# Four shared PSUM banks, VectorE masks and a new order in a four-layer attention kernel

## The chip, the core and the metric

The kernel runs on one core of one Trainium2 chip. The metric is the device time of one execution in microseconds. The core's engines are TensorE (PE in the rows, with its weight loads as PEld), VectorE (DVE), ScalarE (ACT), GpSimd (POOL) and SyncE (SP), which issues most of the DMAs. Matmul results go to PSUM, which has eight banks of 128 partitions by 512 f32; everything else is in SBUF.

## What is computed

Four layers work on x of 8 batches x 256 tokens x 256 features, with a context tensor of the same shape. Each layer adds cross attention (16 heads of 16) and then a feed-forward part to x:

```
x = x + L0_xattn(layernorm(x), ctx)          # causal, strict
x = x + layernorm(x) @ sign(W)
x = x + L1_xattn(layernorm(x), ctx)          # causal
x = x + L1_moe(layernorm(x))                 # 16 experts, top 2, 2 shared
x = x + L2_xattn(ctx, layernorm(x), mask)    # mask of keys, q/k/v normed
x = x + L2_bitlinear_ffn(layernorm(x))       # gate, up, down, quantised
x = x + L3_xattn(layernorm(x), ctx, ctx)     # no weights, no mask
x = x + L3_qlora_ffn(layernorm(x))           # 3 blocks: linear, layernorm, gelu, linear, add
```

An attention is softmax(q k^T / 4 + mask) v for each head. In layer 2 a masked score is replaced by -1e9 in the reference; the kernel adds -1e30 instead.

## The kernel before

**Attention.** A pair of layer and batch, (L, b), is one slot of 16 heads. `ORDER` lists the 32 slots: 16 of layers 0 and 1 mixed, then (2,0) to (2,3), then layer 3 and layer 2 in turn, then the last of layer 3. For each head, TensorE makes the scores twice. The first time (`maxima`, `score_for_max`, L1545) they lie with queries on partitions, and VectorE takes each row's negated maximum from them (`reduce`). These maxima are split into two bf16 parts (L2207, L2209), turned on TensorE (`turn_max`, L1630) and copied by ScalarE as extra rows under the stacked queries (`rows`, L1976). The second time (`score`, `score_for_exp`, L1563) the scores lie with keys on partitions and have the maximum already subtracted; ScalarE takes the exponential (`exp`, L1959), and TensorE multiplies by the values (L1649). Queries and keys are split into three bf16 parts, whose six combinations are stacked on 96 rows by six DMAs each (`q_stack`, `k_stack`, L2789): the high part needs ScalarE alone (`q_hi`), the middle one VectorE as well, the low one GpSimd last. Eight further rows of `k_st` hold ones that pick a head's maximum (`own_rows`, L1983).

**Masks.** In the causal layers VectorE adds a triangle while it takes the maximum: a custom instruction for each half of the keys (L2192), each followed by a read of its accumulator. In layer 2 TensorE adds the mask to the first scores, as one more matmul of an identity by `mask_s`, 512 columns (L1548), and again to the second ones (L1569); VectorE then takes both maxima of a head with one plain reduction (L2196).

**PSUM.** `claim` gives a tile one of the banks of its use: scores ("s") have banks 0 and 1, maxima ("m") banks 2 and 3, all else ("c") banks 4 to 7, with a loan from "m" when 4 to 7 are planned to be full. It takes the bank whose holder is planned to be drained first, and TensorE waits for that drain, in order.

**Norms.** VectorE makes mean and variance (L2090, L2093), GpSimd var+eps, -mean, its power -1/2 and the shift (L2503, L2504, L2506, L2509), ScalarE applies scale and shift (L1910; for the last batch's halves `half_apply`, L2051), TensorE turns the tile. The last batch's three blocks of layer 3 run as two halves of 128 tokens (`last_half`).

**Order.** All engines run through one list of steps: the table `AT` gives each step of each lane a planned time, and `program` visits the steps in the order of those times. Each engine issues its own part of every step in that order. At the start SyncE loads context and x of batch 0, weights for keys and queries, `col`, the value weights and so on; GpSimd makes the constants (`constants`: fills, triangles, numbers) before its first norm; SyncE's zero fills of a scratch table in DRAM (L2839) stand between the first stacks.

## Time and profile before

| | us |
|---|---|
| median of 3 runs (lowest to highest) | 1173.37 (1168.38 to 1174.31) |
| profiled execution, own time | 1173.09 |
| its span, first to last instruction | 1171.4 |
| PE busy in the span | 1061.8 (91%) |
| VectorE busy | 886.7 (76%) |
| ScalarE busy | 810.9 (69%) |
| GpSimd busy | 554.4 (47%) |

A group's busy time is the union of its instructions from start to end. Instructions of TensorE, and of VectorE and ScalarE, overlap: the next one may start before the one ahead has ended, so a row's mean duration is more than it takes of the engine when work is queued. The distance from one start to the next, read from a timeline, is called the pitch below.

### The profile page before, as it was taken

What the parts mean: (1) busy time and instruction counts of PE and PEld (TensorE: products, weight loads), DVE (VectorE), ACT (ScalarE), POOL (GpSimd) and SP (SyncE); (2) the same over time, 40 slices, a digit from 0 to 9 for tenths busy, and PEclk for the clock granted to TensorE, in tenths of its full rate; (3) what the DMA queues carried; (4) which work ended last, traced back from release to release, by engine and by line L of the source; (5) the groups of instructions that cost most, each with busy time, mean ns of one, the idle gap of its engine ahead of it and who ended that gap; (6) DMA issues with size and microseconds to landing.
All of it is one profiled execution on the core that took longest, in us unless ns stands there. A gap on an engine that the chain in (4) does not pass through costs nothing.

```text
span 1171.4 us, 25960 instructions
## 1 busy us (share of the span) xinstructions
PE 1061.8 (91%) x8406; PEld 787.6 (67%) x8406; DVE 886.7 (76%) x2995; ACT 810.9 (69%) x1492; POOL 554.4 (47%) x1111
## 2 busy tenths in 40 slices
PE   5899999999999989888999997899998999889986
PEld 4577777787787867766767664566575765656664
DVE  2898887788465669987847588998888969898643
ACT  5676666666665557566566666567988897899963
POOL 7132364655212456687812126746455445344244
PEclk9899999999999999999999999999999999999898
DMA  8884332225677552522368853322123111322000
GB/s 279 243 287 146 91 92 65 80 74 155 189 217 215 162 151 64 145 73 89 119 194 256 252 186 101 93 62 84 45 75 108 38 55 47 90 64 55 1 19 18
DMA packets 102324, 140.01 MB, mean 120 GB/s; under 512 B 12336, under 2 KB 79792, under 8 KB 102192
## 3 DMA queue, kind: packets, MB, share of 16 engines
q1 hardware_dynamic: 99120, 129.97, 37.8%
q0 software_dynamic: 3072, 8.39, 2.3%
q8 instruction: 70, 1.15, 0.4%
q14 instruction: 62, 0.51, 0.2%
HBM read 65.43 MB, written 22.54 MB: 75 GB/s over the span
## 4 chain that ended last, share of the span: by engine, by line
PE 41%; DVE 22%; ACT 14%; DMA 7%; issue 7%; SPq 5%; POOL 4%; another core or an unknown queue 1%; DVEq 0%; ACTq 0%; POOLq 0%
PE ps L1525 9%; PE ps L1563 4%; PE ps L1649 4%; DVE neg_max L2196 4%; PE ps L1545 4%; DMA w<-in_expert 3%; ACT probs L1959 3%; PE ps L1742 3%; PE ps L1518 3%; DVE ps L2192 2%; PE ps L1532 2%; SPq L2789 2%; DVE bn L2090 2%; ACT q_st L1976 2%; PE ps L1709 2%
## 5 line engine op out<-in xcount | busy, mean ns | idle before, releaser
L1959 ACT ACTIVATE probs<-ps 128x384 f32<-128x384 f32 (+1 forms) x512 | 260.3, 544 | 90.2 <-PE ps L1566 43.5
L1545 PE MATMUL ps<-k_st,q_st 96*128 96x256 bf16 (+1 forms) x1024 | 170.6, 262 | 23.4 <-DVE neg_max L2196 11.8
L1563 PE MATMUL ps<-q_st,k_st 104*128 104x256 bf16 (+1 forms) x1024 | 177.1, 261 | 12.9 <-ACT probs L1959 8.4
L2196 DVE TENSOR_REDUCE neg_max<-ps 128x2 f32<-128x512 f32 x256 | 167.7, 679 | 15.7 <-PE ps L1548 8.9
L1976 ACT ACTIVATE q_st<-ps 8x1024 bf16<-8x1024 f32 x128 | 129.7, 1016 | 42.2 <-PE ps L1630 38.9
L2192 DVE CUSTOM_DVE_ANT_0 ps<-ps,diag_s 128x128 f32<-128x128 f32 (+1 forms) x384 | 123.0, 357 | 29.6 <-PE ps L1545 26.4
L1545 PEld LDWEIGHTS ps<-k_st,q_st 96*128 96x128 bf16 x1024 | 85.4, 98 | 76.4 <-DVE neg_max L2196 23.8
L2503 POOL TENSOR_SCALAR var_eps<-mv 128x2 f32<-128x2 f32 (+1 forms) x115 | 30.7, 267 | 210.1 <-DVE mv L2093 203.2
L1563 PEld LDWEIGHTS ps<-q_st,k_st 104*128 104x128 bf16 x1024 | 90.6, 99 | 58.5 <-ACT probs L1959 20.8
L1649 PE MATMUL ps<-probs,v 128*32 128x256 f32 (+1 forms) x2048 | 122.6, 358 | 2.9 <-ACT probs L1959 1.8
L2569 POOL CAST parts<-qf 128x512 bf16<-128x512 f32 x64 | 39.5, 618 | 115.9 <-DVE qf L2115 57.6
L1649 PEld LDWEIGHTS ps<-probs,v 128*32 128x32 f32 x2048 | 54.4, 109 | 48.3 <-issue 22.6
L2506 POOL TENSOR_TENSOR rstd<-var_eps,neg_half 128x2 f32<-128x2 f32 (+1 forms) x115 | 84.1, 731 | 0.0
L2571 POOL TENSOR_TENSOR parts<-qf,parts 128x512 bf16<-128x512 f32 x64 | 74.5, 1165 | 5.2
L1525 PE MATMUL ps<-w,xn_t 128*128 128x256 f32 x296 | 72.5, 388 | 2.6 <-ACT xn_t L1867 2.4
L1910 ACT ACTIVATE xn<-x,shift,rstd 128x256 f32<-128x256 f32 x112 | 64.1, 633 | 13.8 <-POOL shift L2509 8.0
L1742 PE MATMUL ps<-ring,w 128*128 128x128 f32 x496 | 65.7, 278 | 8.2 <-DMA w<-in_expert 8.1
L2192 DVE DVE_READ_ACCUMULATOR2_ANT neg_max<- 128x1 f32 x512 | 71.8, 140 | 0.0
L1742 PEld LDWEIGHTS ps<-ring,w 128*128 128x128 f32 x496 | 60.9, 191 | 15.2 <-issue 13.8
L1566 PE MATMUL ps<-diag_t,ident_b 128*128 128x256 bf16 x256 | 70.3, 275 | 0.0
L1525 PEld LDWEIGHTS ps<-w,xn_t 128*128 128x128 f32 x296 | 54.4, 193 | 13.0 <-issue 5.5
L1525 PE MATMUL ps<-w,ctx_t 128*128 128x256 f32 x256 | 61.4, 384 | 0.0
(270 smaller groups left out, 2516.3 us busy)
## 6 DMA issues: line engine op xcount, KB each, us to landing
k_st<-parts SPq DMA_DIRECT2D x192, 128.0 KB, 2.4
q_st<-parts SPq DMA_DIRECT2D x192, 128.0 KB
w<-in_expert SPq DMA_DIRECT2D x62, 384.0 KB, 3.9
x_rows<-wo SPq DMA_DIRECT2D x10, 768.0 KB, 7.6
ctx_t<-in_ctx_t SPq DMA_DIRECT2D x16, 256.0 KB, 3.6
ring<-x_rows SPq DMA_DIRECT2D x31, 128.0 KB, 3.4
y_rows<-ring SPq DMA_DIRECT2D x31, 128.0 KB, 3.5
xn_t<-x_rows SPq DMA_DIRECT2D x31, 128.0 KB, 4.0
```

Source lines behind the costliest of these rows:

```text
L1525: last = mm(t[:, a * D:(a + 1) * D], act_t[:, kt, a * P:(a + 1) * P], weight[:, kt, :], start=kt == 0, stop=kt == KT - 1)
L1545: last = mm(t[:, c0:c0 + n], head(q_st, r, h, KROWS, j * P, P), head(k_st, r, h, KROWS, 0, n), start=j == 0 or L != 2, stop=L != 2, skip_g ...
L1563: last = mm(t[:, j * S:j * S + n], head(k_st, r, h, KALL, j * P, P), head(q_st, r, h, KALL, skip, n), start=j == 0 or L == 3, stop=L == 3, ...
L1566: last = mm(t.rearrange("p (j t) -> p j t", j=SJ)[:, :, 0:P], ident_b[:, :], diag_t[:, L, :, :], start=False, stop=True, skip_group_check= ...
L1649: last = mm(t[h4 * DPAD:(h4 + 1) * DPAD, skip:S], v[:, r, j, hg * HPG + h4, :], probs[:, (hg % 2) * HPG + h4, j * S:(j + 1) * S - skip], s ...
L1742: last = mm(t[:, n * P:(n + 1) * P], expert[:, i % RING, c0:c0 + INNER_E], x_tile_t[:, i % 2, kt * P:(kt + 1) * P], start=kt == 0, stop=kt ...
L1959: nc.scalar.activation(probs[:, (hg % 2) * HPG + h4, 0:width], tile_of(key)[:, 0:width], ACT.Exp, scale=SCALE).then_inc(*tile_drained(key))
L1976: nc.scalar.activation(out, tile_of(key)[KROWS:KALL, 0:S].unsqueeze(1).to_broadcast([2 * HPG, HPG, S]), ACT.Copy).then_inc(*tile_drained(key))
L2192: last = V.tensor_tensor_reduce(some, some, diag_s[:, n0:n0 + j * step + 1:step, :], -1.0, -NEG, ALU.add, ALU.min, neg_max[:, hg, h4, j:j ...
L2196: V.tensor_reduce(neg_max[:, hg, h4, :], tile_of(key).rearrange("p (j t) -> p j t", j=SJ), AX.X, ALU.max, negate=True).then_inc(*tile_drai ...
L2506: G.tensor_tensor(rstd[:, kind, tiles], var_eps[:, kind, tiles], neg_half[:, 0:SJ if a is None else 1], ALU.pow).then_inc(*ln_rstd.step((p ...
L2571: G.tensor_tensor(parts[:, 2, n, :, :], rest, parts[:, 1, n, :, :], ALU.subtract).then_inc(*part_lo.step((what, L, b)))
```

## The change

1. `banks`: "s" and "m" both have banks 0 to 3; a loan for "c" may be any of the four.
2. `MASKED_BY_V = range(8)`: in every batch of layer 2 the mask matmul of the first scores is gone, and VectorE adds `mask_s` with the custom instruction, two for each head.
3. At the start: `col` is loaded ahead of the query weights; ten matmuls on the identity (`EARLY`) run before the first product; the three high parts of the first query stack are issued from ScalarE's DMA queue (`stack_hi`); `own_rows` wait for the first query's high part; GpSimd makes the first norm's factors before the triangles, and the numbers after the first query split; context and x of batch 2 are loaded after that split.
4. `apply_by_v` and `half_apply_by_v`: the norm ahead of the last batch's blocks and the norms in its six half blocks are applied by VectorE from mean and power; GpSimd's -mean and shift are gone there.
5. A new table `AT` with other times for all steps.

```diff
+MASKED_BY_V = range(8)
+EARLY = 10
+NORMED_BY_V = {("l3f", LAST)}
...
 def constants(part):
     yield
     part.constants()
+    yield
+    part.masks_causal()
+    yield
+    part.numbers()
...
-        banks = {"s": (0, 1), "m": (2, 3), "c": (4, 5, 6, 7)}
+        banks = {"s": (0, 1, 2, 3), "m": (0, 1, 2, 3), "c": (4, 5, 6, 7)}
...
             pe.wait_ge(*const_ready.at("half"))
+            for _ in range(EARLY):
+                mm(ps[:, 7, 0:P], ident[:, :], ident[:, :], start=True, stop=True)
...
+                    by_pe = L == 2 and b not in MASKED_BY_V
                     last = mm(t[:, c0:c0 + n], head(q_st, r, h, KROWS, j * P, P), head(k_st, r, h, KROWS, 0, n),
-                              start=j == 0 or L != 2, stop=L != 2, skip_group_check=L == 2)
-                if L == 2:
+                              start=j == 0 or not by_pe, stop=not by_pe, skip_group_check=by_pe)
+                if by_pe:
                     last = mm(t, ident_b[:, :], mask_s[:, b % 2, :, :].rearrange("p j t -> p (j t)"),
                               start=False, stop=True, skip_group_check=True)
...
+            def stack_hi():
+                act.wait_ge(*part_hi.at(("q", *ORDER[0])))
+                for at in range(NSPLIT):
+                    if SPLIT_Q[at] == 0:
+                        nc.scalar.dma_start(q_st[at:KROWS:NSPLIT, side(*ORDER[0]), :, :, :].rearrange("d h m t -> d (h m t)"),
+                                            parts[:, 0, PART["q"], :, :].rearrange("p m t -> p (m t)")).then_inc(
+                            *hi_stacked.step(at))
...
                 def own_rows(r):
+                    act.wait_ge(*part_hi.at(("q", 0, 0)))
...
+            def norm_tile(p, b, a, out, src):
+                T = b * SJ + a
+                V.tensor_scalar(out, src, mv[:, 0, T, 0:1], rstd[:, 0, T:T + 1], ALU.subtract, ALU.mult).then_inc(
+                    *norm_by_v.step((p, b, a)))
...
+                    elif L == 2 and b in MASKED_BY_V:
+                        if h == 0:
+                            dve.wait_ge(*mask_ready.at((b, 0)))
+                        for j in range(SJ):
+                            some = tile_of(key)[:, j * S:(j + 1) * S]
+                            last = V.tensor_tensor_reduce(some, some, mask_s[:, b % 2, j, :], -1.0, -NEG,
                                                           ALU.add, ALU.min, neg_max[:, hg, h4, j:j + 1])
                         last.then_inc(*tile_drained(key))
...
+                by_v = a is not None or (p, b) in NORMED_BY_V
+                if not by_v:
+                    G.tensor_scalar(neg_mean[:, kind, tiles], mv[:, kind, tiles, 0], -1.0, None, ALU.mult).then_inc(*ln_mean.step((p, b)))
...
             load_batch(0, 0)
+            load_x(0)
             load_weight(W_L0K)
+            sp.dma_start(col[:, :, :].rearrange("p n k -> p (n k)"), col_d).then_inc(*load["col"].step(0))
             load_weight(W_L0Q)
-            sp.dma_start(col[:, :, :].rearrange("p n k -> p (n k)"), col_d).then_inc(*load["col"].step(0))
```

TensorE at the start, before. `ctx_t` is the context turned, `xn` the normed x, `xn_t` the same turned; the product of `xn_t` and w is the query.

```order
L1518 MATMUL ps<-ctx_t,w 128x256 x4
L1525 MATMUL ps<-w,ctx_t 128x256 x8
L1532 MATMUL ps<-ident,xn 128x128 x4
L1518 MATMUL ps<-ctx_t,w 128x256 x4
L1518 MATMUL ps<-xn_t,w 128x256 x4
L1518 MATMUL ps<-ctx_t,w 128x256 x4
```

TensorE at the start, after:

```order
L1534 MATMUL ps<-ident 128x128 x10
L1539 MATMUL ps<-ctx_t,w 128x256 x4
L1553 MATMUL ps<-ident,xn 128x128 x4
L1539 MATMUL ps<-ctx_t,w 128x256 x4
L1539 MATMUL ps<-xn_t,w 128x256 x4
L1546 MATMUL ps<-w,ctx_t 128x256 x8
L1553 MATMUL ps<-ident,xn 128x128 x4
```

The eight value products (w, ctx_t) stood ahead of the first query product and now stand behind it.

VectorE where layer 2 begins, before. The ISA rows are the custom instruction and the read of its accumulator; `w` holds a token tile here.

```order
L2209 TENSOR_TENSOR max_parts<-neg_max,max_parts 128x2x4
L2196 TENSOR_REDUCE neg_max<-ps 128x2 x2
L2219 RECIPROCAL sum_inv<-ps 128x16
L2222 TENSOR_TENSOR o_tok<-ps,sum_inv 128x2x128
L2196 TENSOR_REDUCE neg_max<-ps 128x2
L2097 TENSOR_TENSOR w<-ps,vec 128x512
```

The same place, after:

```order
L2257 TENSOR_TENSOR max_parts<-neg_max,max_parts 128x2x4
L2240 ISA ps,neg_max<-ps,mask_s 128x256
L2240 ISA neg_max 128x1
L2240 ISA ps,neg_max<-ps,mask_s 128x256
L2240 ISA neg_max 128x1
L2135 TENSOR_TENSOR w<-ps,vec 128x512
```

One reduction of a head has become two custom instructions with two reads, and the token tile's bias comes after the first head and not the third.

TensorE near the end, in layer 3's last slots, before (L1545 is a product for maxima, L1563 one for scores; two of them are one head):

```order
L1545 MATMUL ps<-k_st,q_st 128x256 x4
L1525 MATMUL ps<-w 128x256 x4
L1563 MATMUL ps<-q_st,k_st 128x256 x2
L1660 MATMUL ps<-ident,o_raw 128x128 x4
L1545 MATMUL ps<-k_st,q_st 128x256 x4
```

The same stretch, after (L1567 for maxima, L1585 for scores):

```order
L1585 MATMUL ps<-q_st,k_st 128x256 x2
L1675 MATMUL ps<-probs,v 32x256 x8
L1567 MATMUL ps<-k_st,q_st 128x256 x10
L1553 MATMUL ps<-ident,ring 128x128 x4
L1686 MATMUL ps<-ident,o_raw 128x128 x4
```

No run of one kind was longer than two heads before; now there are runs of three to five heads.

## Rows read from the trace of the kernel before

**Rows 1.** Windows: us; busy and count by engine; granted clock; DMA share; GB/s

```profile
0.00:50.00 50.00, 33.47 (x200) 25.43 (x201) 23.09 (x111) 27.07 (x42) 26.03 (x66) 0.90 0.95 292
50.00:500.00 450.00, 424.75 (x3702) 341.70 (x3702) 345.75 (x1605) 287.94 (x590) 202.10 (x430) 1.00 0.48 140
500.00:700.00 200.00, 185.98 (x1418) 138.00 (x1417) 142.63 (x411) 127.11 (x262) 91.11 (x203) 1.00 0.56 168
700.00:1000.00 300.00, 271.01 (x2028) 179.31 (x2028) 261.71 (x597) 238.74 (x385) 162.92 (x273) 0.98 0.26 74
1000.00:1100.00 100.00, 92.48 (x764) 63.88 (x764) 87.35 (x205) 91.33 (x144) 38.21 (x70) 0.98 0.19 53
1100.00:1171.40 71.40, 54.09 (x299) 39.30 (x297) 26.20 (x72) 38.72 (x73) 34.00 (x71) 0.90 0.04 16
```

**Rows 2.** Windows of L1548 (mask matmuls) alone: us; PE and PEld busy

```profile
500.00:700.00 200.00, 24.30 (x64) 6.14 (x64) 1.00 0.56 168
700.00:1000.00 300.00, 24.82 (x64) 6.27 (x64) 0.98 0.26 74
```

**Rows 3.** Groups by form: count, then busy us, mean ns, idle before

```profile
L2192 DVE DVE_READ_ACCUMULATOR2_ANT neg_max<- 128x1 f32 x512 | 71.8, 140 | 0.0
```

**Rows 4.** Timeline of PE: start, us, what, count

```profile
905.28 0.38 PE L1548 MATMUL ps<-mask_s,ident_b 128*128 128x512 bf16 x1
905.50 2.21 PE L1781 MATMUL ps<-w,xn_t 128*128 128x512 bf16 x8
```

**Rows 5.** Timeline of VectorE, a causal head and a plain reduction

```profile
94.93 0.47 DVE L2192 CUSTOM_DVE_ANT_1 ps<-ps,diag_s 128x256 f32<-128x256 f32 x1
95.31 0.14 DVE L2192 DVE_READ_ACCUMULATOR2_ANT neg_max<- 128x1 f32 x1
95.31 0.33 DVE L2192 CUSTOM_DVE_ANT_0 ps<-ps,diag_s 128x128 f32<-128x128 f32 x1
...
946.52 0.68 DVE L2196 TENSOR_REDUCE neg_max<-ps 128x2 f32<-128x512 f32 x1
947.11 0.68 DVE L2107 TENSOR_TENSOR qf<-qf,parts 128x512 f32<-128x512 f32 x1
```

**Rows 6.** Waits, whole span: total us, times, longest

```profile
PE ps L1545 <- DVE neg_max L2196: 11.8, 19, 1.5
...
PE ps L1742 <- DMA w<-in_expert: 8.1, 11, 1.4
...
PE ps L1563 <- ACT probs L1959: 8.4, 11, 2.2
```

**Rows 7.** Timeline of the first 29 us

```profile
5.43 0.12 POOL L2482 MEMSET score<- 128x32 f32 x1
...
6.64 3.51 PE L1518 MATMUL ps<-ctx_t,w 128*128 128x256 f32 x8 [6.64 <-DMA w<-in_w]
...
10.81 0.19 POOL L2509 TENSOR_TENSOR shift<-neg_mean,rstd 128x2 f32<-128x2 f32 x1
...
15.61 1.89 PE L1518 MATMUL ps<-xn_t,w 128*128 128x256 f32 x8
...
19.30 3.88 ACT L1983 ACTIVATE k_st<-own 8x1024 bf16<-8x1024 bf16 x4
19.30 6.04 SPq L2789 DMA_DIRECT2D q_st<-parts  x6
...
28.01 0.49 PE L1545 MATMUL ps<-k_st,q_st 96*128 96x128 bf16 x4 [0.26 <-DMA q_st<-parts]
```

**Rows 8.** Timeline of one half block's norm near the end

```profile
1160.28 0.57 POOL L2506 TENSOR_TENSOR rstd<-var_eps,neg_half 128x1 f32<-128x1 f32 x1
...
1160.92 0.19 POOL L2509 TENSOR_TENSOR shift<-neg_mean,rstd 128x1 f32<-128x1 f32 x1
1161.15 0.60 ACT L2051 ACTIVATE w<-w,shift,rstd 128x256 f32<-128x256 f32 x1 [3.04 <-POOL shift L2509]
```

**Rows 9.** Groups by form: the nearest forms of a VectorE norm

```profile
L2394 DVE TENSOR_SCALAR xn_t<-xn 128x256 bf16<-128x256 f32 x16 | 4.9, 351 | 0.0
```

More of the change, by code:

```diff
@@ L760, in norm @@
     yield
-    part.apply(p, b)
+    if (p, b) in NORMED_BY_V:
+        part.apply_by_v(p, b)
+    else:
+        part.apply(p, b)
     yield
@@ L1131, in last_half @@
         yield
-        part.half_apply(n, a)
+        part.half_apply_by_v(n, a)
         yield
@@ L1357, in normed_of, with wait_hi_stacked @@
             return h_of(b) if p == "l3f" else xn[:, NORMED[p], :, :]
+        def wait_hi_stacked(eng):
+            eng.wait_ge(*hi_stacked.at(max(at for at, part in enumerate(SPLIT_Q) if part == 0)))
         def half(a):
@@ L1876, in split_hi @@
                     act.wait_ge(*stacked[what][side(*order[-1])].at((*order[-1], NSPLIT - 1)))
+                    if what == "q" and order[-1] == ORDER[0]:
+                        wait_hi_stacked(act)
                 order.append((L, b))
@@ L1923, in q_hi @@
                     split_hi("q", L, b)
+                    if (L, b) == ORDER[0]:
+                        stack_hi()
                 def token_hi(what, b):
@@ L2155, in v_take @@
                 def v_take(L, b):
+                    if L == 0 and b < 2:
+                        dve.wait_ge(*const_ready.at("v"))
                     before = same_side_before(L, b)
@@ L2456, in half_bias, with half_apply_by_v, apply_by_v @@
                     V.bn_aggr(mv[:, 0, T, :], bn[:, 0, T, :]).then_inc(*ln_moments.step((("y", n), LAST, a)))
+                def half_apply_by_v(n, a):
+                    dve.wait_ge(*ln_rstd.at((("y", n, a), LAST)))
+                    y = y_set(LAST)[0][:, a, :]
+                    norm_tile(("y", n), LAST, a, y, y)
+                def apply_by_v(p, b):
+                    dve.wait_ge(*ln_rstd.at((p, b)))
+                    for a in range(SJ):
+                        norm_tile(p, b, a, normed_of(p, b)[:, a, :], x[:, b * SJ + a, :])
                 def half_add(n, a):
@@ L2783, in stack @@
                     wait_filled(sp, ("s", *before, HG - 1, HPG - 1))
-                n = 0
+                n = split.count(0) if (what, L, b) == ("q", *ORDER[0]) else 0
                 for part, ready in enumerate((part_hi, part_mid, part_lo)):
+                    if part == 0 and n:
+                        continue
                     sp.wait_ge(*ready.at((what, L, b)))
```

36 lines of the change are left out of this document (24 added, 12 removed), and 1054 rows, old and new, of the table AT.

## The prediction

> **What bounds the kernel now.** I read the windows first, since the shares of the whole span hide that the stretches differ [rows 1]. From 50 to 500 us TensorE is busy 94% of the time and VectorE 77%. From 500 to 700, where layer 2's first four batches lie beside the experts, TensorE is busy 93%, VectorE 71% and ScalarE 64%: TensorE alone is full. From 700 to 1000, with the other four batches of layer 2, TensorE has 90%, VectorE 87% and ScalarE 80%; from 1000 to 1100 the three have 92%, 87% and 91%. There no engine is far ahead, and a lighter TensorE soon meets the two others. The first 50 us keep TensorE busy for 33.5 only, with the DMA engines at 0.95, and the last 71.4 for 54.1: these two ends are chains of dependent steps. Then I read the timelines, because a busy TensorE is not a TensorE at its peak. A mask matmul starts at 905.28 and lasts 0.38 us, yet the next matmul starts at 905.50 [rows 4]: in a queue it takes 0.22 us. VectorE overlaps in the same way: a custom instruction over 256 columns starts at 94.93, the next one at 95.31, and the accumulator's read lies beside that next one; a plain reduction over 512 columns starts at 946.52 and what follows it at 947.11 [rows 5]. So the pitches are 0.38 and 0.59 us.
>
> **Masks on VectorE.** TensorE loses 64 matmuls in each of the two stretches [rows 2], at 0.22 us each 14.1 us, 28.2 in all. The recorded durations would make it 49.1, the sum of the two busy times, which is an upper bound that the pitch speaks against. VectorE's price is read from the causal head, since the trace has no such instruction in layer 2: the form is the same, PSUM in and out with a bf16 operand beside it. A head goes from 0.59 to 2 x 0.38 = 0.76 us, 0.17 more, and for 128 heads 21.8 us, 10.9 in each stretch. The upper end takes all durations in a row: 2 x (0.47 + 0.14) - 0.68 = 0.54 a head, 69 us in all [rows 3, 5]. The lower end is zero, since the custom form touches every score that the reduction touches. I take the pitch, the nearest row.
>
> What of this is on the path depends on the stretch. From 500 to 700 VectorE's 142.6 us become 153.5 and stay well under TensorE, whose 186.0 fall to 171.9. I let three quarters of the 14.1 shorten the stretch, -10.5; the rest goes to waits for expert weights, of which TensorE has 8.1 us in all already [rows 6]. From 700 to 1000 VectorE would have 261.7 + 10.9 = 272.6 of 300 and TensorE 256.9, so VectorE becomes the fullest engine. Here I count a quarter of TensorE's gain and a quarter of VectorE's load: -3.5 + 2.7 = -0.8. The sum is -11.3, with ends of -28 (all of TensorE's time comes off, VectorE costs nothing) and +11 (nothing comes off, VectorE's second half counts in full).
>
> Here two pages of the Trainium skill give other prices. The page "TensorE: Matmul & The Clock Gate", section "Back-to-back issue gap", gives about 131 ns as the sustained spacing of matmuls with 512 columns; by that the 128 masks would be worth 16.8 us and the whole forecast would come out some 5 us later. The trace does not agree: it shows 0.22 us, in a stream of eight further matmuls of 512 columns too, 2.21 us for eight. The other page's rule stands with the first rival.
>
> **Shared banks.** TensorE's own waits that this can touch are those for VectorE's maxima, 11.8 us, and for ScalarE's exponentials, 8.4 us [rows 6]. With four banks a run of three to five heads of one kind can be in flight where two could be. But a wait ends when the reader is done, and more banks don't make the reader faster; what they remove is the part due to uneven runs. I take a fifth, -4. The ends are -20 (both waits gone) and +8: TensorE claims in order, by planned drain times, and a bank held by a late exponential can now stop a product for maxima, which at worst doubles the shorter of the two waits. Nothing is added behind such a wait but TensorE's own queue.
>
> **The start.** The chain to the first maxima now: the first product begins at 6.64 with the key weights' landing; the first norm's factors are ready at 11.0, although GpSimd ends its fills at 5.55 and needs some 1.5 us for them; the query product runs from 15.61 to 17.5, behind the eight value products; SyncE issues the six query stacks from 19.30 to 25.34; the first maxima start at 28.01, when the last stack has landed [rows 7]. After: the factors are ready near 7.2; ScalarE applies them while the first product runs, TensorE turns x at about 10.3, makes the second key product, and the query product ends near 14. That is 3.4 us earlier. Three of six stacks leave from ScalarE, so SyncE issues three, some 3 us instead of 6. The first maxima could start at 21 to 22, 6 to 7 us earlier. The zero fills that filled the DMA engines during the second stack come later. What it costs: ScalarE makes its eight `own_rows` in one piece, twice the 3.88 us of the row, and the norm of batch 1 and the exponentials queue behind its three DMA issues and these rows; the fills and weights still have to move, with the DMA engines at 0.95 now. I take -5 of the 7; the ends are -8 and 0. The ten early matmuls lie in time in which TensorE waits for weights. Eight products took 3.51 us at 6.64 and 1.89 at 15.61, near the ratio of the clock's two levels (2.4 and 1.2 GHz), so if the early ones raise the clock the first product ends up to 1.6 us sooner; that is inside the ends. The triangles are due only at the first maxima, and about 2.5 us of GpSimd's work hides beside the first products.
>
> **The end.** In a half block GpSimd's power ends at 1160.85, the shift at 1161.11 and ScalarE's norm at 1161.75, 0.90 us after the power [rows 8]. VectorE's norm has no row; the nearest is a tensor_scalar of the same 128x256 from f32 at 351 ns [rows 9], with bounds of 0.3 (its pitch) and 0.6 (as slow as ScalarE). With 0.1 for the hand-over it ends 0.45 after the power, and the power starts 0.18 earlier without -mean: 0.63 saved. Four such norms stand one after another (the one ahead of the blocks, three blocks), -2.6, with ends -4 and 0. VectorE is busy 26 of 71 us there, so it has the room; its adds for the other half queue behind the wait for the power, which they need anyway.
>
> **Sum.** -11.3 - 4 - 5 - 2.6 = -22.9 against the profiled execution's own 1173.09, which lies 0.3 from the median: 1150.2 us.
>
> **Rival 1, VectorE becomes the bound (slower).** If a masked head costs the durations and not the pitch, 0.54 us more, then VectorE has 261.7 + 34.6 = 296 us to do from 700 to 1000. It is at 87% there now; at 90% that takes 329 us, +29. With -5 from 500 to 700, -5 at the start and -2.6 at the end it is +16: 1189. It decides from about 0.35 us more a head. For it: a new read of the accumulator sits ahead of every split of the maxima. Against it: the overlap in [rows 5]. The page "VectorE: DVE Perf Modes", section "The DRAIN you can't avoid", says that the next VectorE instruction does not start until the pipe is empty; by that rule this rival would hold, but the trace shows the next one 0.09 us ahead of the recorded end. I give it 0.12.
>
> **Rival 2, the middle is bound by more than TensorE.** The mask matmuls go, and ScalarE, VectorE and the expert weights keep their pace, so that only the ends move: -5 - 2.6 = -7.6, 1165.5. For it: ScalarE at 80 to 91% after 700 and VectorE at 87%. Against it: 500 to 700, where TensorE alone is full. 0.19.
>
> **Rival 3, the change does not do what it says.** The earlier start is lost by 50 us because the same loads and fills are only moved, and longer runs of one kind make the banks a wait in turn, +8 against the masks' -11: the sum is about -3, 1170. For it: the DMA share at the start. 0.07.
>
> **How the numbers follow.** The forecast, 1150.2, has a chance of 0.62, and its own range from the terms' ends is 1132 to 1163. Rival 2 spreads over 1161 to 1171. The range 1132 to 1176 takes in the forecast, rivals 2 and 3 and leaves out rival 1 and a little on both sides. A measurement of this kernel tells about 0.5%, 5.9 us, from no change. Faster by more: 0.62 of the forecast and 0.11 of rival 2, 0.73. Within: 0.08 of rival 2 and 0.07 of rival 3, 0.15. Slower: 0.12.
>
> **What would show it.** In the new profile the first maxima start near 21.5 us; a masked head on VectorE has custom starts 0.38 apart; the matmul count is 128 lower but for ten; the stretch that held 500 to 700 is some 10 us shorter and that of 700 to 1000 hardly; VectorE is over 90% there; from the last exponential to the end 2 to 4 us are gone. A start of the maxima after 26, a head at 1.2 us, or a TensorE wait for maxima above 20 us would each break one step. What would make it wrong as a whole is the new table: it moves every step, and a place where an engine's order no longer fits what is ready costs several us at once and shows in no single row of before.

## The result and the profile after

The changed kernel takes **1195.19 us** (median of 4 runs, 1192.96 to 1199.67) against 1173.84 of before: a ratio of 1.0173, 95% interval 1.0134 to 1.0212. It is 21 us slower where the forecast said 23 faster and put its top end at 1176. The profiled execution has its own time of 1192.96 us and a span of 1191.2.

Time is compared here at equal work. Each head has one exponential, 512 in all, 16 to a slot; their numbers from 0 mark how far a kernel has come. Windows of before and then of after, each from exponential 0 to 256 (layers 0 and 1), from 256 to the last (layers 2 and 3, the experts), and from the last to the end; columns as in [rows 1]:

```profile
35.80:518.40 482.60, 451.14 (x3948) 359.60 (x3946) 373.16 (x1724) 309.45 (x629) 219.39 (x472) 0.99 0.49 145
518.40:1116.90 598.50, 549.01 (x4173) 380.92 (x4171) 481.00 (x1165) 460.33 (x793) 286.64 (x521) 0.98 0.34 100
1116.90:1171.40 54.50, 38.90 (x193) 28.90 (x191) 20.89 (x56) 24.07 (x50) 25.64 (x57) 0.93 0.04 15
```

```profile
30.60:538.80 508.20, 462.45 (x3949) 365.58 (x3949) 372.50 (x1745) 307.59 (x632) 221.92 (x477) 0.98 0.48 143
538.80:1139.90 601.10, 521.00 (x4008) 363.37 (x4047) 499.24 (x1520) 459.12 (x790) 286.28 (x522) 0.99 0.35 100
1139.90:1191.20 51.30, 36.84 (x184) 27.95 (x184) 23.07 (x59) 19.90 (x42) 21.90 (x40) 0.97 0.04 16
```

The first exponential comes 5.2 us earlier and the last stretch is 3.2 shorter, as forecast. But layers 0 and 1, where behind the start only the banks and the order differ, take 25.6 us more for the same matmuls (3948 and 3949): TensorE idles 45.8 of 508.2 us instead of 31.5 of 482.6, and its busy time grows by 11.3. In the second stretch TensorE is busy 28.0 us less, and the stretch is 2.6 us longer: all of it became idle time. That this is just the 28.2 that the masks were priced at is in part chance, since order and clock differ too. Where the masks are the only difference in the program, the same stretch has 542.44 us of TensorE in e2 and 521.00 in after, 21.4 less, and 549.01 in before and 534.29 in e9 (below), 14.7 less at a lower clock.

The waits of TensorE in after over the whole span (total us, times, longest), the rows that answer to [rows 6] and the largest others:

```profile
PE ps L1553 <- ACT xn L1946: 8.5, 9, 2.4
PE ps L1656 <- DVE max_parts L2257: 7.5, 14, 1.3
PE ps L1567 <- DMA q_st<-parts: 7.3, 4, 3.7
PE ps L1768 <- DMA w<-in_expert: 6.7, 10, 1.5
PE ps L1585 <- DVE neg_max L2240: 6.1, 8, 2.3
PE ps L1585 <- DVE neg_max L2232: 5.7, 11, 1.2
PE ps L1585 <- ACT probs L1997: 5.5, 11, 1.3
PE ps L1567 <- DVE neg_max L2240: 4.9, 11, 1.4
```

L1553 turns the normed x, L1656 the maxima's parts, L1768 is a product of the experts, L1567 the product for maxima, L1585 the scores' product, L2232 and L2240 VectorE's causal and masked maxima. That L1585 waits for VectorE's maxima is new, since the two kinds now share their banks: before has no such row, while e5, with the banks alone, has 1.4 us of them and after 14.0. All of TensorE's waits for VectorE's maxima together are 16.2 us in before and 23.1 in after; over 20 was the prediction's own sign that a step had broken. The longest wait of these rows is 3.7 us. Summed over all rows of this view by the engine waited for, TensorE waits in before for VectorE 30.8 us in 61 waits, for ScalarE 41.4 in 64 and for DMAs 20.5 in 19; in after for VectorE 61.5 us in 107 waits, for ScalarE 45.0 in 69 and for DMAs 15.7 in 16.

**The new table forecasts the direction itself.** Its times are tenths of a microsecond of the planner's own model. Exponential 256 is planned at 4969 in the old table and at 5065 in the new one, the last at 10715 and 10783: 9.6 us and 6.8 us later by the plan's own account, and its last step is 3.7 us later. Measured are 20.4, 23.0 and, at the end, 19.9.

### The profile page after: what moved, and what is told of

It is laid out like the page before. It is cut to its first block, busy times and chain, and to the rows that moved or that the text cites. A ratio compares the mean times of both kernels' runs of the same rounds, so it can differ in the third digit from the quotient of the medians.

```text
span 1191.2 us, 26150 instructions
## 1 busy us (share of the span) xinstructions
PE 1043.8 (88%) x8257; PEld 776.1 (65%) x8298; DVE 908.9 (76%) x3387; ACT 804.2 (68%) x1484; POOL 551.1 (46%) x1097
## 4 chain that ended last, share of the span: by engine, by line
PE 39%; DVE 26%; ACT 11%; issue 8%; DMA 6%; POOL 5%; SPq 4%; another core or an unknown queue 0%; DVEq 0%; POOLq 0%; ACTq 0%
PE ps L1546 9%; PE ps L1675 4%; DVE ps L2232 4%; PE ps L1585 4%; PE ps L1768 3%; PE ps L1567 3%; ACT probs L1997 3%; DVE ps L2240 3%; PE ps L1539 3%; DVE bn L2123 2%; DMA w<-in_expert 2%; PE ps L1553 2%; SPq L2863 2%; DVE neg_max L2244 2%; PE ps L1775 2%
## 5 line engine op out<-in xcount | busy, mean ns | idle before, releaser
L1997 ACT ACTIVATE probs<-ps 128x384 f32<-128x384 f32 (+1 forms) x512 | 256.4, 548 | 75.6 <-PE ps L1588 31.4
L1585 PE MATMUL ps<-q_st,k_st 104*128 104x256 bf16 (+1 forms) x1024 | 172.4, 262 | 26.6 <-DVE neg_max L2240 6.1
L1567 PE MATMUL ps<-k_st,q_st 96*128 96x256 bf16 (+1 forms) x1024 | 156.8, 264 | 24.2 <-DMA q_st<-parts 7.3
L2014 ACT ACTIVATE q_st<-ps 8x1024 bf16<-8x1024 f32 x128 | 129.6, 1016 | 54.5 <-PE ps L1656 48.9
L2232 DVE CUSTOM_DVE_ANT_0 ps<-ps,diag_s 128x128 f32<-128x128 f32 (+1 forms) x384 | 123.0, 360 | 25.8 <-PE ps L1567 21.2
L1585 PEld LDWEIGHTS ps<-q_st,k_st 104*128 104x128 bf16 x1024 | 89.2, 99 | 72.5 <-issue 20.3
L1567 PEld LDWEIGHTS ps<-k_st,q_st 96*128 96x128 bf16 x1024 | 84.9, 99 | 71.9 <-issue 21.4
L2240 DVE CUSTOM_DVE_ANT_0 ps<-ps,mask_s 128x256 f32<-128x256 f32 x256 | 101.1, 453 | 10.7 <-PE ps L1567 8.9
L2244 DVE TENSOR_REDUCE neg_max<-ps 128x2 f32<-128x512 f32 x128 | 82.7, 680 | 11.7 <-PE ps L1567 11.6
L1675 PEld LDWEIGHTS ps<-probs,v 128*32 128x32 f32 x2048 | 54.9, 109 | 52.2 <-issue 28.1
L1768 PE MATMUL ps<-ring,w 128*128 128x128 f32 x496 | 66.3, 279 | 8.7 <-DMA w<-in_expert 6.7
L2232 DVE DVE_READ_ACCUMULATOR2_ANT neg_max<- 128x1 f32 x512 | 72.5, 142 | 0.0
L1768 PEld LDWEIGHTS ps<-ring,w 128*128 128x128 f32 x496 | 61.0, 191 | 14.9 <-issue 11.6
```

Of the source, the lines that this page charges most:

```text
L1567: last = mm(t[:, c0:c0 + n], head(q_st, r, h, KROWS, j * P, P), head(k_st, r, h, KROWS, 0, n), start=j == 0 or not by_pe, stop=not by_pe, ...
L1585: last = mm(t[:, j * S:j * S + n], head(k_st, r, h, KALL, j * P, P), head(q_st, r, h, KALL, skip, n), start=j == 0 or L == 3, stop=L == 3, ...
L1675: last = mm(t[h4 * DPAD:(h4 + 1) * DPAD, skip:S], v[:, r, j, hg * HPG + h4, :], probs[:, (hg % 2) * HPG + h4, j * S:(j + 1) * S - skip], s ...
L1768: last = mm(t[:, n * P:(n + 1) * P], expert[:, i % RING, c0:c0 + INNER_E], x_tile_t[:, i % 2, kt * P:(kt + 1) * P], start=kt == 0, stop=kt ...
L1997: nc.scalar.activation(probs[:, (hg % 2) * HPG + h4, 0:width], tile_of(key)[:, 0:width], ACT.Exp, scale=SCALE).then_inc(*tile_drained(key))
L2014: nc.scalar.activation(out, tile_of(key)[KROWS:KALL, 0:S].unsqueeze(1).to_broadcast([2 * HPG, HPG, S]), ACT.Copy).then_inc(*tile_drained(key))
```

## The experiments

All are timed against runs of before on the same chip, four chips in all. The mean granted clock differs from run to run, and the time goes with it: 95 runs of before lie between 0.969 and 0.987, and their time falls by 8.0 us for each 0.01 (correlation -0.81). So the table has two columns of differences to before: of the medians, and from one straight-line fit over the runs of all kernels (8.1 us for each 0.01), with 95% bounds: the difference that is left when the clock is the same. Where a change itself lowers the clock, as is seen below, the last column leaves that part of its cost out, so both are needed.

| kernel | median us | ratio, 95% | difference | clock, median | at equal clock |
|---|---|---|---|---|---|
| after | 1195.19 | 1.0173, 1.0134 to 1.0212 | +21.4 | 0.974 | +17.9 ± 2.3 |
| e1 after, old order | 1184.58 | 1.0073, 1.0042 to 1.0104 | +9.1 | 0.970 | +4.1 ± 1.6 |
| e2 after, masks by TensorE | 1200.11 | 1.0192, 1.013 to 1.0254 | +24.6 | 0.978 | +24.5 ± 2.3 |
| e3 new order and banks | 1207.18 | 1.0255, 1.0188 to 1.0321 | +31.7 | 0.981 | +32.7 ± 2.3 |
| e4 masks alone | 1183.06 | 1.0055, 1.003 to 1.008 | +7.6 | 0.971 | +1.8 ± 1.6 |
| e5 banks alone | 1173.06 | 0.9982, 0.9953 to 1.001 | -1.8 | 0.981 | +0.3 ± 1.4 |
| e6 end alone | 1174.30 | 1.0005, 0.9969 to 1.0041 | -0.5 | 0.978 | -0.9 ± 1.4 |
| e7 new order only from 257 on | 1184.53 | 1.0071, 1.004 to 1.0102 | +9.7 | 0.978 | +7.9 ± 1.5 |
| e8 as e1, masks by TensorE | 1183.00 | 1.0042, 1.0008 to 1.0076 | +8.2 | 0.974 | +3.0 ± 1.5 |
| e9 no masks on either engine | 1176.13 | 1.0007, 0.9981 to 1.0034 | +0.3 | 0.972 | -3.6 ± 1.5 |
| e10 masks on both engines | 1183.69 | 1.0085, 1.0058 to 1.0113 | +7.8 | 0.976 | +7.5 ± 1.4 |
| e11 VectorE masks four batches | 1178.08 | 1.0035, 1.0006 to 1.0064 | +2.2 | 0.975 | +2.5 ± 1.4 |
| e12 new order up to 256 | 1198.33 | 1.023, 1.017 to 1.029 | +22.5 | 0.968 | +16.8 ± 2.2 |
| e13 new order up to 128 | 1188.50 | 1.0137, 1.0066 to 1.0208 | +12.0 | 0.972 | +9.9 ± 2.3 |
| e14 new order 128 to 256 | 1200.77 | 1.0219, 1.0148 to 1.029 | +24.2 | 0.966 | +16.2 ± 2.5 |
| e15 start and end | 1176.80 | 0.9998, 0.9968 to 1.0028 | +0.3 | 0.978 | +1.1 ± 1.5 |
| e16 banks and end | 1171.90 | 0.997, 0.993 to 1.0009 | -4.6 | 0.980 | -1.5 ± 1.5 |

And the start of some exponentials in the profiled executions, in us in before and as differences to it. Each row is one execution: that of e4 is 3.5 us slower than its median, that of e1 4.7 faster.

| kernel | 0 | 16 | 64 | 128 | 160 | 256 | 448 | last | end |
|---|---|---|---|---|---|---|---|---|---|
| before | 35.8 | 56.3 | 127.0 | 240.4 | 289.9 | 518.4 | 1008.9 | 1116.9 | 1171.4 |
| after | -5.3 | +0.4 | +9.6 | +4.8 | +13.7 | +20.4 | +21.9 | +23.0 | +19.9 |
| e1 | -5.2 | +0.4 | +0.5 | 0.0 | +0.5 | +1.4 | +9.5 | +7.1 | +6.8 |
| e3 | 0.0 | +6.4 | +16.0 | +12.2 | +19.1 | +24.7 | +32.3 | +33.0 | +33.8 |
| e4 | +0.2 | -2.6 | -2.5 | -3.2 | -4.0 | -3.0 | +14.9 | +13.2 | +13.5 |
| e12 | -5.1 | -3.8 | +5.9 | +5.2 | +12.7 | +17.6 | +24.2 | +21.9 | +21.6 |
| e14 | -5.3 | +1.1 | +1.2 | +2.9 | +13.8 | +18.8 | +28.5 | +26.1 | +25.8 |

**First four: which part costs.** T1 held that the masks and banks pay and the order takes it away; T2 that the masks cost as well.

e1: the changed kernel with the order of before from the 9th exponential on. The old times are shifted to join the new start, so that no step changes its place behind it.

```diff
-    (267, 278, 287, 291, 296, 300, 304, 328, 376, 379, 382, 385, 407, 410, 413, 416, 483, 489, 497, 502, 518, 521, 524, 527,
+    (267, 278, 287, 291, 296, 300, 304, 328, 376, 379, 379.004, 379.008, 379.019, 394, 397, 410, 431, 434, 444, 447, 480,
```

> The changed kernel whole (four shared banks, masks on VectorE, new start, VectorE's last norms), but the steps stand in the order of the table of before from the ninth exponential on; only what lies ahead of it keeps the new order. Theory 1, the new order is what costs: the time falls from 1195 to 1155 to 1170, and the first half (up to the 257th exponential, 538.8 us in the changed kernel, 518.4 before) ends before 522. Theory 2, the masks or the shared banks cost under any order: the time stays at 1185 to 1200.

e2:

```diff
-MASKED_BY_V = range(8)
+MASKED_BY_V = ()
```

> The changed kernel with layer 2's masks made by TensorE again for all eight batches, nothing else. Theory 1, the order costs and the masks are worth little either way: 1189 to 1201, and the first half is as in the changed kernel, 538 to 540 us. Theory 2, the masks on VectorE cost: 1180 or less. The prediction's own step (masks on VectorE save 11 us) expects 1206.

e3: the kernel before with the new table and the shared banks. In e5 the same line of banks is all that differs from before.

```diff
-        banks = {"s": (0, 1), "m": (2, 3), "c": (4, 5, 6, 7)}
+        banks = {"s": (0, 1, 2, 3), "m": (0, 1, 2, 3), "c": (4, 5, 6, 7)}
```

> The kernel before with two things alone: the new table and the four shared banks (the new table's runs of one kind don't fit two banks). The start, the masks and the last norms are as before. Theory 1, the order costs: 1190 to 1205, with the first half ending 18 us or more later than before's 518.4. Theory 2, other parts cost: within 8 us of before's 1173.

e4: the kernel before with VectorE's masks.

```diff
+                    by_pe = L == 2 and b not in MASKED_BY_V
...
-                if L == 2:
+                if by_pe:
```

> The kernel before with one thing alone: VectorE adds layer 2's masks. Theory 1 takes the masks for nearly free or a small gain: 1163 to 1176. Theory 2, they cost: 1180 or more. The prediction's step expects 1162.

The old order takes 11 us off the changed kernel (e1) and the new one adds over 30 to before (e3): the order is the largest cost. But e1 is still 9 us slower than before, and the masks alone make before 7.6 us slower (e4). Under the new order the same masks are worth -4.9 (e2 against after; with four runs of each this is clear of zero only at equal clock, -6.6 ± 3.2). So the parts don't simply add, and T1 is half right: it fails on the masks. At equal clock e4's loss is 1.8 ± 1.6: most of the 7.6 comes with a lower clock.

**Second four: banks, end, the second half of the order.**

> The kernel before with nothing changed but the banks: scores and maxima share four. Theory A (the new order is what costs in layers 0 and 1; shared banks cost nothing by themselves): with the old order the exponential number 256 starts within 2 us of before (518.4), the time is 1168 to 1176. Theory B (the shared banks are the loss in layers 0 and 1, since a bank held by a late exponential stops a product for maxima): number 256 starts 10 us or more later and the time is 1183 or more. The prediction's step said -4, with ends of -20 and +8.

e6, with the norm ahead of the blocks changed in the same way:

```diff
-        part.half_apply(n, a)
+        part.half_apply_by_v(n, a)
```

> The kernel before with the last norms on VectorE and nothing else changed. From the last exponential to the end before takes 54.5 us. Theory A (each of the four norms in the chain is shorter by about 0.6 us): 51 to 52.5, the time 1170 to 1172. Rival (the chain is bound by GpSimd's power and VectorE's statistics, so the norm's engine does not matter, and the 51.4 us of after come from elsewhere): 54 to 55 us, time as before within 1 us.

e7, from the second lane of the table (the exponentials) around number 256, against the new table:

```diff
-4985, 5004, 5018, 5065, 5097, 5102, 5107
+4843, 4856, 4860, 4910.012, 4910.023, 4910.028, 4910.03
```

> The changed kernel in full, but from the 9th to the 256th exponential with the order of before, and from the 257th on with the new order. Theory A (the new order costs about 24 us before exponential 256 and is better than the old one after it, where it is 598 to 601 us against 604 in e1): exponential 256 starts at 518 to 522 and the time is 1170 to 1178. Theory C (the cost of the new order is only put off, work left undone by then comes after it): 1185 or more.

e8: e1 with `MASKED_BY_V = ()`, as in e2.

> As e1_old_order (new start, shared banks, last norms on VectorE, order of before from the 9th exponential on), but TensorE adds layer 2's masks as before. Theory A (masks on VectorE cost here what they cost alone in e4 less what shared banks give back, 5 to 8 us, and the new start is worth nothing by 56 us): 1167 to 1174. Theory D (the masks are not the cost of e1; the new start or the banks are): 1180 or more.

Banks alone move exponential 256 by 0.9 us and the time by nothing that can be told: theory B falls. The end alone is worth 0.4 us from the last exponential to the end in the trace (54.1 us), not 2.6: that is e6's rival, and its theory A falls. e7 has exponential 256 at 519.2 as theory A said, but with 1184.5 it is above A's 1178 and just under C's 1185, and no better than e1 (3.8 ± 2.1 worse at equal clock): the new order behind exponential 256 brings nothing either. e8, 1183.0, is where theory D put it, 1180 or more: under the old order the masks are not the cost of e1, from which e8 differs by 1.6 us, 1.1 ± 2.0 at equal clock. Banks, start and end together cost 8.2 us, although banks alone (e5), end alone (e6) and start with end (e15, below) cost nothing that can be told. At equal clock 3.0 ± 1.5 are left of it; why they cost in company stays open.

**Third four: the masks taken apart, and the order.**

e9: VectorE's branch of e4 is never taken, and TensorE's matmuls stay away. e10: VectorE adds, and TensorE too. e11: half the batches.

```diff
-                    elif L == 2 and b in MASKED_BY_V:
+                    elif False:
```

```diff
-                    by_pe = L == 2 and b not in MASKED_BY_V
+                    by_pe = L == 2
```

```diff
-MASKED_BY_V = range(8)
+MASKED_BY_V = range(4)
```

> The kernel before, but layer 2's maxima are taken without the masks: neither TensorE's 128 mask matmuls nor VectorE's adds are done, VectorE keeps its plain reductions (what is left out: the mask's part of the maximum; the masks of the scores stay). The price of the matmuls by themselves. Theory E (after exponential 288 TensorE is not alone the limit: what it no longer does becomes waits for VectorE and ScalarE, and a lower clock): 1167 to 1176. Theory F (the prediction's: the pitch of 0.22 us comes off where TensorE is full): 1155 to 1163.

> The kernel before, TensorE adds layer 2's masks as before and VectorE adds them once more (a masked score is masked twice, the maximum is the same). VectorE's price with TensorE's load unchanged. Theory E (VectorE's queue is the limit after exponential 288, so TensorE's matmuls there are covered, and the clock stays as in before): as e4, 1178 to 1186, with a clock of 0.975 or more. Theory F (TensorE is the limit and VectorE's 0.17 us a head is mostly covered): 1175 to 1179 if e4's loss is not VectorE's; a time 8 us or more above e4 would say that the matmuls do sit on the path.

> The kernel before, with VectorE adding the masks of layer 2's first four batches only (64 heads, beside the experts, where VectorE is busy 71%). Theory E (the loss of e4 lies after exponential 384 or so, where VectorE is as full as TensorE; before it, VectorE has room): 1165 to 1174, clock 0.975 or more. Rival (any wait that TensorE gains lowers its clock, so this half costs as well): 1177 to 1181.

e12, the second lane around number 256, against the new table:

```diff
-4985, 5004, 5018, 5065, 5097, 5102, 5107
+4985, 5004, 5018, 5062.003, 5062.005, 5062.006, 5062.008
```

> The changed kernel in full, with the new order up to the 256th exponential and the order of before behind it: the counterpart of e7. Theory A (the new order's cost is made before exponential 256, about 20 us, and the old order behind it costs what it costs in e1, 604 us): exponential 256 at 538 to 541 and 1195 to 1202. Theory C (work is only shifted between the halves, so that halves from two orders cost at the seam as e7 may have): exponential 256 at 538 to 541, and 1185 to 1194.

This settles the masks. **In the old order, taking TensorE's 128 mask matmuls away brings nothing**: with them gone and nothing put in their place, the time is 1176.1 against 1175.9 (e9). VectorE's adds cost 7.8 us with TensorE's load unchanged (e10), and 7.3 with the matmuls gone (7.6 of e4 less 0.3 of e9). Windows from exponential 288 to 448, layer 2's masked heads beside experts and layer 3, of before, e9 and e4:

```profile
610.80:1008.90 398.10, 363.56 (x2759) 249.45 (x2760) 329.41 (x767) 304.47 (x521) 183.80 (x305) 0.99 0.37 108
```

```profile
613.40:1013.40 400.00, 352.21 (x2673) 240.20 (x2674) 332.01 (x767) 304.90 (x521) 184.09 (x305) 0.97 0.37 108
```

```profile
610.50:1023.90 413.40, 359.14 (x2641) 246.12 (x2674) 343.09 (x1025) 305.28 (x522) 184.28 (x305) 0.95 0.36 105
```

e9 has 86 matmuls fewer than before, TensorE's busy time falls by 11.4 us, its idle time grows by 13.3, and the clock goes from 0.99 to 0.97. In e4 the busy time hardly falls, although the matmuls are gone, since the others run at 0.95. Where that happens is seen in windows of 5 us at the same time, before and then e4; both start at exponential 320, and by 745 before has begun 332 and e4 328:

```profile
725.00:730.00 5.00, 2.94 (x29) 1.37 (x22) 4.83 (x11) 2.19 (x5) 3.56 (x5) 1.00 0.65 170
730.00:735.00 5.00, 2.98 (x21) 1.36 (x19) 4.76 (x12) 4.46 (x9) 4.63 (x8) 1.00 0.13 42
735.00:740.00 5.00, 4.63 (x45) 3.22 (x46) 4.72 (x10) 3.62 (x7) 4.01 (x5) 1.00 0.05 11
740.00:745.00 5.00, 5.00 (x52) 3.60 (x53) 4.90 (x11) 3.69 (x7) 3.28 (x4) 1.00 0.66 181
```

```profile
725.00:730.00 5.00, 2.73 (x27) 1.40 (x16) 4.83 (x11) 1.72 (x4) 4.01 (x5) 1.00 0.66 184
730.00:735.00 5.00, 2.54 (x15) 1.15 (x14) 4.79 (x10) 3.73 (x8) 4.70 (x8) 0.66 0.09 26
735.00:740.00 5.00, 4.60 (x33) 2.74 (x32) 4.79 (x9) 1.93 (x4) 2.17 (x3) 0.50 0.00 0
740.00:745.00 5.00, 5.00 (x20) 3.31 (x19) 3.61 (x6) 3.70 (x7) 2.01 (x2) 0.50 0.38 102
```

In both VectorE is busy 4.8 of 5 us for 10 us and TensorE only a little over half. In before TensorE's waits there are for VectorE, the two longest being these:

```profile
729.69 0.39 PE L1545 MATMUL ps<-k_st,q_st 96*128 96x256 bf16 x2 [1.48 <-DVE neg_max L2196]
731.92 0.39 PE L1545 MATMUL ps<-k_st,q_st 96*128 96x256 bf16 x2 [0.82 <-DVE neg_max L2196]
```

So VectorE is the bound there. In e4 TensorE is busy a little less still, and then its clock is granted at 0.50, 1.2 GHz, while its work comes back: 20 matmuls in 5 us instead of 52. The clock's part is carried by the timed runs too: with the matmuls kept it is 0.977 (before, same chip) and 0.976 (e10) in the median, with them gone 0.972 (e9) and 0.971 (e4). At equal clock the matmuls would be worth 3.6 us (e9 against before) to 5.7 (e4 against e10); the lower clock takes 0.005 x 8.1 us per 0.01, some 4, back. That fewer matmuls cause the lower clock rests on these pairs; e1 against e8 and after against e2 point the same way (0.971 and 0.974, 0.974 and 0.978), but not beyond their spread.

e11 shows that the first four batches cost too (+2.2), though VectorE has room there by the windows [rows 1]: the rival with its 1177 to 1181 is right, theory E's 1165 to 1174 wrong. e12 loses most of what after loses up to exponential 256 (+17.6 of +20.4), and then 4.0 more; its 1198.3 is theory A's.

**Last four: where the order costs.**

e13 and e14, the second lane around numbers 128 and 256, against the new table; e14 has the old order up to 128 as e1:

```diff
-2247, 2260, 2349, 2357, 2360, 2377, 2380
+2247.001, 2260, 2349, 2353.006, 2356, 2372, 2383
```

```diff
-4985, 5004, 5018, 5065, 5097, 5102, 5107
+4835, 4854, 4868, 4912.003, 4912.005, 4912.006, 4912.008
```

> The changed kernel in full, with the new order up to the 128th exponential only and the order of before behind it. The traces of after and e12 have gone 8 us back between exponentials 48 and 64 and then gained 2 to 5 again by 128. Theory G (the cost is spread, each part of the order carries its own, and what is behind by 128 stays behind): exponential 256 starts 3 to 8 us later than in e1 (519.8), time 1186 to 1192. Theory H (the loss by 128 is work drawn forward, which the old order behind it gets back): as e1, 1182 to 1186. Theory I (one late step early on makes all of the loss): 1195 or more.

> The changed kernel in full, with the new order from the 128th to the 256th exponential only. In after this stretch, from 240.4 + 4.8 to 518.4 + 20.4, is 15.6 us longer than in before, in two steps of 9 at exponentials 144 to 160 and 224 to 240. Theory G: exponential 256 starts 12 to 17 us later than in e1, time 1194 to 1202. Theory H: 1182 to 1188. With both parts additive, the sum of the two losses is that of e12 against e1, 14 us.

e15, against e8:

```diff
-        banks = {"s": (0, 1, 2, 3), "m": (0, 1, 2, 3), "c": (4, 5, 6, 7)}
+        banks = {"s": (0, 1), "m": (2, 3), "c": (4, 5, 6, 7)}
```

> The order of before from the 9th exponential on, separate banks, masks by TensorE, and only the new start and VectorE's last norms. Theory A (the new start brings the first exponential 5 us forward, and the DMA engines, full until 56 us in either kernel, give it back; the end is worth 1): 1172 to 1178. Rival J (the new start costs by what it moves, as the difference of e8, e5 and e6 has it, +4): 1177 to 1181. The prediction's steps (-5 and -2.6): 1165 to 1170.

e16: the edits of e5 and e6 together.

> The kernel before with shared banks and VectorE's last norms, the order, the masks and the start of before: the parts that cost nothing by themselves. If they add, -1 to -2 us, 1171 to 1176, which a measurement can't tell from none; a gain over 6 us would say that the two help each other.

Against e1, the new order costs 3.9 us up to 128, 16.2 from 128 to 256 and 13.7 in both; at equal clock 5.8 ± 2.7, 12.1 ± 2.7 and 12.7 ± 2.5. So the two parts are not additive: their sum is 20.1, and 14 was expected. Exponential 256 moves against e1 by 4.3, 17.4 and 16.2 us. Neither part is made good by the old order behind it, so theory H falls; theory G stands for 128 to 256, and the early part is the smaller (with its four runs it is clear of zero at equal clock alone). The old order and the new one in that stretch, e1 and then e14, both from exponential 128 to 256 with the same 2190 matmuls within 5:

```profile
240.40:519.90 279.50, 257.55 (x2185) 208.69 (x2184) 205.36 (x937) 172.68 (x369) 132.10 (x281) 0.99 0.51 147
```

```profile
243.30:537.20 293.90, 266.27 (x2190) 215.08 (x2190) 207.06 (x944) 172.79 (x370) 132.66 (x282) 0.96 0.48 138
```

Of the 14.4 us, 5.7 are idle time of TensorE (22.0 and 27.6) and 8.7 more busy time at a clock of 0.96 instead of 0.99. Exponentials 144 to 160 alone take 35.3 us in e14 and 23.2 in e1. Windows of 3 us from e14 there:

```profile
277.00:280.00 3.00, 1.37 (x18) 0.91 (x20) 2.93 (x20) 1.38 (x2) 2.33 (x9) 0.85 0.03 5
280.00:283.00 3.00, 3.00 (x21) 2.36 (x12) 1.66 (x10) 1.20 (x3) 1.04 (x5) 0.58 0.00 0
...
289.00:292.00 3.00, 1.95 (x17) 1.39 (x15) 1.02 (x5) 0.67 (x2) 1.32 (x2) 1.00 0.98 335
292.00:295.00 3.00, 1.89 (x7) 1.55 (x8) 2.97 (x13) 2.31 (x4) 0.95 (x3) 0.63 0.81 303
```

This stretch holds 266 matmuls instead of 207, so part of its 12 us is work that the table places here and takes out elsewhere: e14 is 2.9 us behind before at 128, 13.8 at 160 and 6.5 again at 192. What stays is what the windows show: TensorE is busy for half of 277 to 280, where it waits 1.9 us for a stack of queries in flight, and for two thirds of 289 to 295, where it waits 0.9 us and then 1.2 for VectorE's maxima; both times its clock falls right behind. After goes back in several such clusters, by 8 us between exponentials 48 and 64, by 9 between 144 and 160, by 9 between 192 and 224 and by 9 between 224 and 240, with gains of 4 to 7 in between, and not by one late step. Which property of the new table makes the clusters stays open: it wasn't tried with separate banks, since its runs of one kind need four, nor in pieces shorter than 120 exponentials.

e15 puts the start at nothing in the old order: 0.9998. The trace of after says why. The query product, the query stacks' issue on both queues, ScalarE's own rows and the first product for maxima, answering to [rows 7]:

```profile
11.93 1.89 PE L1539 MATMUL ps<-xn_t,w 128*128 128x256 f32 x8
...
14.49 1.96 ACTq L1901 DMA_DIRECT2D q_st<-parts  x3
...
15.88 1.84 SPq L2863 DMA_DIRECT2D q_st<-parts  x3
...
19.07 7.65 ACT L2022 ACTIVATE k_st<-own 8x1024 bf16<-8x1024 bf16 x8
...
20.95 0.66 PE L1567 MATMUL ps<-k_st,q_st 96*128 96x128 bf16 x6
```

The maxima start at 20.95 instead of 28.01, as forecast. Then exponentials 0 to 16, before and after:

```profile
35.80:56.30 20.50, 16.81 (x170) 11.65 (x168) 16.71 (x87) 13.35 (x24) 3.98 (x4) 0.92 0.76 249
```

```profile
30.60:56.70 26.10, 20.61 (x175) 14.36 (x174) 13.77 (x73) 12.66 (x25) 5.19 (x6) 0.80 1.00 335
```

The DMA engines are at 1.00 and TensorE waits 3.7 us in one piece for the next query stack; the clock is 0.80. In before their share there is 0.76, so e15's theory, which has them full in either kernel, is right on the time alone. In e12, which starts as after does, 3.8 us of the gain are left at exponential 16, so the size of this loss is not the same each time. Over all traces with the old order there, exponential 16 starts at 53.7 to 56.3 us with the old start and at 56.8 to 57.5 with the new one: nothing is gained by then. With the new order it starts at 62.8 with the old start (e3) and at 52.5 to 57.5 with the new one (after, e2, e12, e13): there the start does give something.

## Why the prediction was wrong

**The table had no term.** This is the step that failed first: the sum took the new order at nothing. The working moved steps only where masks, banks, start and end touch them. It named the table as what would make it wrong as a whole, but gave it neither a price nor a chance, and so the range ended at 1176. The table costs 10.6 us in after (against e1; 13.8 ± 2.7 at equal clock) and over 30 on the kernel before (e3 against e5), for whose steps it wasn't planned. The table's own times for the same exponentials stood in the diff and were later than the old ones by 9.6 and 6.8 us; they should have been compared first.

The other terms can be counted in two ways, both at equal clock and both ending at after's +17.9. With the order last: +3.0 for banks, start and end (e8), +1.1 for the masks on top (e1), +13.8 for the order. With the order early: +0.3 for the banks (e5), +32.4 for the order on top (e3), -8.2 ± 3.2 for start and end (e2 against e3), -6.6 ± 3.2 for the masks (after against e2). The forecast had -4 for the banks, -7.6 for start and end, -11.3 for the masks and nothing for the order. So in the changed kernel's own company start and end are worth what was forecast and the masks over half, while in the old order both are worth nothing or cost. The table is the one term that is large and of the wrong sign either way. What is given for e2 and e3 rests on four runs each.

The range, too, was narrower than the working: the terms' own ends add up to 1113 and 1192, and no step leads from them to 1132 and 1163.

**Masks, -11.3: too much anywhere, and wrong in sign in the old order.** In the changed kernel they are worth -4.9 (e2 against after), in the kernel before +7.6 (e4). The price of a masked head was right. VectorE's timeline in e4:

```profile
851.58 0.43 DVE L2202 CUSTOM_DVE_ANT_0 ps<-ps,mask_s 128x256 f32<-128x256 f32 x1
851.92 0.14 DVE L2202 DVE_READ_ACCUMULATOR2_ANT neg_max<- 128x1 f32 x1
851.92 0.47 DVE L2202 CUSTOM_DVE_ANT_0 ps<-ps,mask_s 128x256 f32<-128x256 f32 x1
852.31 0.14 DVE L2202 DVE_READ_ACCUMULATOR2_ANT neg_max<- 128x1 f32 x1
852.31 0.69 DVE L2122 TENSOR_TENSOR x<-ps,ctx_n 128x512 f32<-128x512 f32 x1
```

The head takes 0.73 us (0.34 and 0.39), the forecast 0.76. So rival 1, which needed the durations, is not what happened: again the next instruction starts before the recorded end of the one ahead. The prediction set beside it the Trainium skill's page "VectorE: DVE Perf Modes", section "The DRAIN you can't avoid", and took from it only that the next instruction waits for the empty pipe; the same section adds that a next one that is not held starts earlier, and the 0.34 and 0.39 us here agree with that. The price of a mask matmul, 0.22 us, was read from one; the stream of eight that the prediction called on as well, 2.21 us, has its starts (2.21 - 0.38) / 7 = 0.26 us apart. Off TensorE's busy time came 28.0 us in after, but 21.4 between e2 and after and 14.7 between before and e9, where the clock fell. What failed is the step "what of this is on the path". It read the fullest engine of a stretch of 200 or 300 us as the one that sets its length, and let three quarters of 14.1 us count. e9 gives +0.3 for both stretches together (-3.6 ± 1.5 at equal clock). On a scale of 5 us VectorE is full at 725 to 735 and TensorE waits for it, and from 740 to 745 TensorE is full; what TensorE no longer does in the former becomes idle time, and then a lower clock. VectorE's 21.8 us count with 7.8 (e10), above the 2.7 that were allowed. Rival 2, which let only the ends move, had the right reason for the masks (the middle is bound by more than TensorE) but no price for VectorE's adds, and its ends gave nothing either in the old order.

**Shared banks, -4:** -1.8 alone, +0.3 ± 1.4 at equal clock, inside the ends -20 and +8. That banks and masks help each other isn't shown. From exponential 288 to 448 the masked kernel takes 413.4 us with separate banks (e4) and 404.6 with shared ones (e1), but this compares an execution of e4 that is 3.5 us above its median with one of e1 that is 4.7 below; e5, with shared banks and TensorE's masks, takes 404.6 as well. At equal clock the masks cost 1.8 ± 1.6 with separate banks and 1.1 ± 2.0 with shared ones.

**Start, -5:** the first maxima are at 20.95 (forecast 21 to 22), the first exponential is 5.2 us early, and in the old order nothing is left by exponential 16. That is rival 3's first half, "lost by 50 us because the same loads and fills are only moved". The term's own sentence named the DMA share of 0.95 and kept 5 of 7 all the same.

**End, -2.6:** the norm is as forecast. In after:

```profile
1182.52 0.56 POOL L2566 TENSOR_TENSOR rstd<-var_eps,neg_half 128x1 f32<-128x1 f32 x1
...
1183.11 0.41 DVE L2130 TENSOR_SCALAR w<-w,mv,rstd 128x256 f32<-128x256 f32 x1 [0.51 <-POOL rstd L2566]
```

It ends 0.44 us after the power; in [rows 8] it was 0.90. But alone (e6) the stretch behind the last exponential loses 0.4 us, and the time changes by -0.9 ± 1.4 at equal clock. The other traces tell what the 3.2 of after are. With the old order at the end, that stretch takes 54.5 to 54.9 us with the old norms and 53.9 to 54.2 with VectorE's. With the new order there it takes 55.3 with the old norms (e3, one trace) and 51.4 to 51.5 with VectorE's (after, e2, e7). So the norms are worth some 0.7 us in the old order and 3.9 in the new one, around the forecast 2.6. The gain of after needs both.

**No version beats before by more than can be told.** e16, banks and end on the kernel before, is the fastest with 0.997 (0.993 to 1.0009).

## What to carry to other kernels

Take work off an engine only where it is the last to finish on the scale of single steps: read windows of a few microseconds and who waits for whom, since the fullest engine over hundreds of microseconds may be idle half of just those places. An order table is a change of its own with its own price; where it carries planned times, compare those of old and new at the same step before anything else, and give the table a term and a chance. Test each part alone and in company: here the same masks were worth +7.6 us alone, +1.6 with the rest of the change but the order, and -4.9 with all of it; at equal clock +1.8 ± 1.6, +1.1 ± 2.0 and -6.6 ± 3.2, so that only the order's part in this is clear.

## What the hardware showed

The mean granted clock of one and the same program differs by up to 0.018 between executions (0.969 to 0.987 over 95 runs on four chips), and 0.01 goes with 8 us of 1175, so that effects of 5 us need ten runs and the clock beside each time. Removing matmuls can lower the clock of those that stay: median 0.971 without the 128 mask matmuls (e4), 0.976 with them (e10). The waits ahead of a fall need not be long: in e4 the granted clock goes from 1.00 (730 to 731) by 0.81 (731 to 732) to 0.50, and TensorE's waits from 725 to the fall are 0.8, 1.5 and 0.5 us, among short groups of matmuls; a wait of 1.9 us follows when it has already fallen.
